# Output projection of the layers: one fp32 product against three products of high and low parts

## The reference, cut to what matters

```python
h = shift_token(x)
q, k, v = split(h @ wqkv)                  # 3 x 512 columns, 8 heads of 64
q, k = l2norm(q) * qs, l2norm(k) * ksc
q, k = rotary_xpos(q, k)
o = local_attention(q, k, v)               # windows of 128 tokens: own and previous
x = x + o @ wo                             # wo: 512 x 256, the product that is changed
h = layernorm(shift_token(x)) * lg + lb
h = h @ w1 + b1
x = x + (a * gelu(g)) @ w2 + b2
```

## Time and profile before

| | us |
|---|---|
| median of 3 runs (2383.41 to 2384.18) | 2384.12 |
| the profiled execution | 2385.16 |
| its span in the trace | 2383.4 |
| granted clock of PE, mean over the span | 0.982 |
| busy time PE / DVE / ACT / POOL | 2254.4 / 1928.0 / 1509.0 / 602.5 |

### The profile page before, as it was taken

One profiled execution on the slowest core, in us unless ns is written; L12 is line 12 of the kernel. 1 busy time (PEld: TensorE's weight loads), 2 busy tenths in 40 slices (PEclk: granted clock), 3 DMA queues, 4 the chain that ended last, 5 costly groups with the idle time before them and its releaser, 6 DMA issues. The chain is left out here.

```text
span 2383.4 us, 61531 instructions
## 1 busy us (share of the span) xinstructions
PE 2254.4 (95%) x21120; PEld 1735.2 (73%) x21120; DVE 1928.0 (81%) x4501; ACT 1509.0 (63%) x2970; POOL 602.5 (25%) x667
## 2 busy tenths in 40 slices
PE   6999999999999999789999998799999999987898
PEld 4776776777677766567777776688777777765787
DVE  6999799979998999678888886466688888873886
ACT  5777577757776777267767775344577776763343
POOL 1000000000000000145555552122355555441332
PEclk9999999999999999899999999899999999999999
DMA  4100100010011000300000000100100000001110
GB/s 127 34 13 20 60 15 14 19 60 15 19 50 42 15 20 19 122 1 1 9 0 9 1 8 1 56 0 0 50 1 8 1 9 0 9 1 36 54 35 27
DMA packets 67271, 58.43 MB, mean 25 GB/s; under 512 B 4069, under 2 KB 64605, under 8 KB 66913
## 3 DMA queue, kind: packets, MB, share of 16 engines
q1 hardware_dynamic: 67168, 57.07, 7.7%
HBM read 44.47 MB, written 8.40 MB: 22 GB/s over the span
## 5 line engine op out<-in xcount | busy, mean ns | idle before, releaser
L599 ACT ACTIVATE at_p<-at_ps_s,at_shift 128x1024 f32<-128x1024 f32 (+3 forms) x384 | 335.6, 899 | 90.6 <-PE at_ps_s L800 49.9
L340 DVE TENSOR_TENSOR at_p_lo<-at_p,at_p_hi 128x1024 f16<-128x1024 f32 (+3 forms) x384 | 356.9, 950 | 5.5
L1374 ACT ACTIVATE ly_probs<-ly_masked,ly_small,ly_rq 128x256 f32<-128x256 f32 x512 | 301.9, 595 | 8.4 <-DVE ly_small L1608 8.0
L1213 POOL TENSOR_TENSOR ly_rope_a<-ly_rope_a,ly_rope_t 128x512 f32<-128x512 f32 x128 | 163.6, 1278 | 318.7 <-DVE ly_rope_t L1576 318.7
L828 PE MATMUL at_ps_o<-at_v,at_p_hi 128*128 128x65 f16 x2304 | 238.4, 193 | 3.4 <-DVE at_p_lo L340 2.5
L828 PEld LDWEIGHTS at_ps_o<-at_v,at_p_hi 128*128 128x128 f16 x2304 | 210.8, 96 | 39.3 <-issue 26.8
L829 PE MATMUL at_ps_o<-at_v,at_p_hi 128*128 128x64 f16 x2304 | 237.5, 194 | 0.0
L830 PE MATMUL at_ps_o<-at_v,at_p_lo 128*128 128x65 f16 x2304 | 236.4, 192 | 0.0
L1605 DVE CUSTOM_DVE_ANT_0 ly_masked<-ly_ps,ly_mask 128x256 f32<-128x256 f32 x512 | 195.8, 419 | 48.8 <-PE ly_ps L1896 29.5
L335 DVE CAST at_p_hi<-at_p 128x1024 f16<-128x1024 f32 (+3 forms) x384 | 206.1, 554 | 25.9 <-ACT at_p L599 14.4
L1382 ACT ACTIVATE ly_operands_plain<-ly_ps 128x512 f32<-128x512 f32 x256 | 153.4, 599 | 112.8 <-PE ly_ps L1907 97.9
(11 more groups left out here) (241 smaller groups left out, 6230.5 us busy)
## 6 DMA issues: line engine op xcount, KB each, us to landing
at_w_raw<-in_Wv SPq DMA_DIRECT2D x32, 128.0 KB, 2.2
at_w_raw<-in_Wq SPq DMA_DIRECT2D x32, 128.0 KB, 2.3
at_w_raw<-in_Wk SPq DMA_DIRECT2D x32, 128.0 KB, 2.3
at_xio<-in_states SPq DMA_DIRECT2D x4, 1024.0 KB, 6.6
ly_a_raw<-x SPq DMA_DIRECT2D x8, 512.0 KB, 4.0
out<-stream SPq DMA_DIRECT2D x16, 256.0 KB, 2.2
ly_shifted<-stream SPq DMA_DIRECT2D x8, 508.0 KB
x<-at_xio SPq DMA_DIRECT2D x3, 1024.0 KB, 4.4
```

What stands on the lines that cost most here:

```text
L340: dve.tensor_tensor(p_lo[u % P_RING][:, :, off:], probs[u % P_RING][:, :, off:], p_hi[u % P_RING][:, :, off:], ALU.subtract).then_inc(p_lo ...
L599: act.activation(probs[u % P_RING][:, :, off:], ps_s[u % 2][:, :, off:], ACT.Exp, bias=shift[:], scale=SCORE_SCALE).then_inc(exp_done, 1)
L1213: pool.tensor_tensor(ra[:, i, :], ra[:, i, :], rt[:, i, :], ALU.add).then_inc(s["add_done"], 1)
L1374: step = act.activation(pr[:, j % 2, h, :], sm[:, j % 2, h, :], ACT.Exp, bias=small[:, j % 2, 1, h:h + 1], scale=rq[:, par, 2 * j + h:2 * ...
```

## The change

The output projection is done with three fp32r products per k-step instead of one fp32 product. For that

- wo is split into `wo_hi` and `wo_lo` once per layer, by POOL (`split_out_weights`, a cast and a subtraction of 128 x 1024) behind its tile 0; PE's wait ahead of tile 1 is for this split (`wo_done`) instead of for the transfer;
- DVE's `normalise_out` writes a plain `o_full`; ACT copies it to the high part (`high_out`, behind `exps(0)` of the next tile); POOL subtracts for the low part (`low_out`, first thing of the next tile, ahead of `add_rotated`); `oT_done` is now POOL's;
- PE does `project_out(t-1)` behind `project(t+2, 1)` instead of ahead of `probs_T(0)`;
- DVE does `add_attended(t-1)` behind `maxima(3)` instead of behind `maxima(2)`;
- a few semaphores that only ordered what was ordered anyway go, and buffers are laid out anew in the same memory.

```diff
+        wo_hi, o = cut(o + 8, LP, D)
...
-        oT, o = cut(o, LP, P, of=plain)
-        wo, o = cut(o, LP, D, of=plain)
+        oT, o = cut(o, 2, LP, P)
+        o_full, o = cut(o, LP, P, of=plain)
+        wo_raw, _ = cut(o, LP, D, of=plain)
+        wo_lo, o = cut(o, LP, D)
...
+                def low_out(g):
+                    hold(pool, s["tick"], (s["o_hi"], at(g + 1)))
+                    pool.tensor_tensor(oT[:, 1], o_full, f32(oT[:, 0]), ALU.subtract).then_inc(s["oT_done"], 1)
+
+                def split_out_weights(l):
+                    hold(pool, s["tick"], (s["ld_wo"], 16 * l + 16))
+                    pool.tensor_copy(wo_hi, wo_raw).then_inc(s["wo_hi"], 1)
+                    after(pool, "wo_hi", l + 1)
+                    pool.tensor_tensor(wo_lo, wo_raw, f32(wo_hi), ALU.subtract).then_inc(s["wo_done"], 1)
...
+                    if not first:
+                        low_out(nth(l, t) - 1)
                     if left >= 1:
                         add_rotated(l, t + 1, 0)
                         add_rotated(l, t + 1, 1)
...
-                        tile(l, t, t % 2, (t + 3) % TB)
+                        tile(l, t, t % 2, (t + 3) % TB, first=t == 0)
+                        if t == 0:
+                            split_out_weights(l)
...
+                def high_out(g):
+                    hold(act, s["tick"], (s["o_full"], at(g + 1)), (s["wo_mm"], at(g)))
+                    act.activation(oT[:, 0], o_full, ACT.Copy).then_inc(s["o_hi"], 1)
...
                     exps(l, t, 0, par)
+                    if not first:
+                        high_out(g - 1)
...
-                    after(dve, "wo_mm", g)
-                    dve.tensor_tensor(oT.rearrange("p j q -> p (j q)"), ps_pv[:], rT, ALU.mult).then_inc(s["oT_done"], 1)
+                    after(dve, "oT_done", g)
+                    dve.tensor_tensor(o_full.rearrange("p j q -> p (j q)"), ps_pv[:], rT, ALU.mult).then_inc(s["o_full"], 1)
...
                     maxima(l, t, 2, par)
-                    if not first:
-                        add_attended(l, t - 1)
                     if left >= 1:
                         rotate_k(l, t + 1, w)
                     maxima(l, t, 3, par)
+                    if not first:
+                        add_attended(l, t - 1)
...
-                        step = pe.matmul(ps_misc[:, 0:D], oT[:, k, :], wo[:, k, :], start=(k == 0), stop=(k == LP - 1),
-                                         skip_group_check=True)
+                        step = three_products(pe, ps_misc[:, 0:D], oT[:, 0, k, :], oT[:, 1, k, :], wo_hi[:, k, :], wo_lo[:, k, :],
+                                              k == 0, k == LP - 1)
...
-                    if not first:
-                        project_out(l, t - 1)
                     probs_T(g, 0)
                     if left >= 2:
                         project(l, t + 2, par, 1)
+                    if not first:
+                        project_out(l, t - 1)
                     probs_T(g, 1)
...
-                            hold(pe, s["tick"], (s["ld_wo"], 16 * l + 16))
+                            hold(pe, s["tick"], (s["wo_done"], at(l + 1)))
```

More of the change, by code:

```diff
@@ L1081, in phase_layers @@
                  "mx_done nb_done h_lo rc_done rB_done oT_done red_done fl_done ra_done kn_done kT_done xa_done msk "
-                 "kz_done ca_in ca_out pw_done add_done xs_done "
-                 "warmed bn ag vr nr xnd fT_mm ff_done f_hi f_lo gu_mm gl_done uf_done u_hi u_lo y_mm ya_done pw2 "
+                 "kz_done ca_in ca_out pw_done add_done xs_done o_full o_hi wo_hi wo_done "
+                 "bn ag vr nr xnd fT_mm f_hi f_lo gu_mm gl_done uf_done u_hi u_lo y_mm ya_done pw2 "
                  "b2_done z_gated z_done yg_done out_done tick")
@@ L1086, in phase_layers @@
         PE_SEMS = "xT_mm qkv_mm sc_mm pt_mm pv_mm qkT_mm rT_mm wo_mm fT_mm gu_mm y_mm"
[L1087 to L1090, removed]
+        ACT_SEMS = "o_hi h_hi ex_done sq_done pt_done rT_done qT_done v_done w_hi_done f_hi gl_done"
+        DVE_SEMS = ("mx_done nb_done h_lo rc_done rB_done o_full red_done fl_done ra_done kn_done kT_done xa_done msk "
+                    "w_lo_done bn ag vr nr xnd f_lo uf_done u_lo ya_done yg_done")
+        POOL_SEMS = "oT_done wo_hi wo_done aw_hi aw_done rope_next fw_hi fw_done xs_done kz_done ca_in ca_out pw_done add_done u_hi pw2 b2_done"
         def start(eng, which):
@@ L1186, in _ @@
                 pool.memset(f32(carry[:]), 0.0).then_inc(s["zeroed"], 1)
-                pool.memset(expo[:], -0.5).then_inc(s["const_done"], 1)
-                pool.wait_ge(s["zeroed"], 1)
+                pool.memset(expo[:], -0.5).then_inc(s["zeroed"], 1)
+                pool.wait_ge(s["zeroed"], 2)
                 def carry_in(l, t, par, w):
@@ L1237, in split_attention_weights, with tile @@
                     pool.tensor_tensor(a_lo[:, cols], a_raw[:, cols], f32(a_hi[:, cols]), ALU.subtract).then_inc(s["aw_done"], 1)
-                def tile(l, t, par, w, left=NT):
+                def low_out(g):
[6 more added lines that the diff above has]
+                    pool.tensor_tensor(wo_lo, wo_raw, f32(wo_hi), ALU.subtract).then_inc(s["wo_done"], 1)
+                def tile(l, t, par, w, left=NT, first=False):
+                    if not first:
+                        low_out(nth(l, t) - 1)
                     if left >= 1:
@@ L1256, in tile @@
                         inverse_deviation(l, 0)
+                    if left == 0:
+                        low_out(nth(l, t))
                 def chunk(l, c, left=NCH):
@@ L1384, in copy_reciprocals @@
                 def copy_reciprocals(g):
-                    hold(act, s["tick"], (s["rT_mm"], at(g + 1)), (s["oT_done"], at(g)))
+                    hold(act, s["tick"], (s["rT_mm"], at(g + 1)), (s["o_full"], at(g)))
                     act.activation(rT, ps_pt[:], ACT.Copy).then_inc(s["rT_done"], 1)
+                def high_out(g):
+                    hold(act, s["tick"], (s["o_full"], at(g + 1)), (s["wo_mm"], at(g)))
+                    act.activation(oT[:, 0], o_full, ACT.Copy).then_inc(s["o_hi"], 1)
                 def chunk_full(l, c, src):
@@ L1392, in chunk_full @@
                     for k in range(KT):
-                        step = act.activation(ffull[:, k, :], src[k][:], ACT.Identity,
+                        act.activation(ffull[:, k, :], src[k][:], ACT.Identity,
                                               scale=lncol[:, 0, k:k + 1], bias=lncol[:, 1, k:k + 1])
-                    step.then_inc(s["ff_done"], 1)
                 def chunk_hi(l, c, par, src):
@@ L1414, in u_high, with tile @@
                     act.activation(uT[rows_of, i, 0, :], uf[rows_of, i % 2, :], ACT.Copy).then_inc(s["u_hi"], 1)
-                def tile(l, t, par, slot, left=NT):
+                def tile(l, t, par, slot, left=NT, first=False):
                     g = nth(l, t)
                     exps(l, t, 0, par)
+                    if not first:
+                        high_out(g - 1)
                     if left >= 2:
@@ L1432, in tile @@
                     if left == 0:
-                        after(act, "warmed", 2 * l)
-                        act.activation(warm[:], expo[:, 0:1], ACT.Gelu).then_inc(s["warmed"], 1)
+                        act.activation(warm[:], expo[:, 0:1], ACT.Gelu)
                     copy_probs(g, 2)
@@ L1441, in tile @@
                     copy_reciprocals(g)
+                    if left == 0:
+                        high_out(g)
                     if left == 1:
@@ L1481, in last_chunk @@
                         return
-                    after(act, "warmed", 2 * l + 1)
-                    act.activation(warm[:], expo[:, 0:1], ACT.Exp).then_inc(s["warmed"], 1)
+                    act.activation(warm[:], expo[:, 0:1], ACT.Exp)
                     squares(l + 1, 0, 1)
@@ L1509, in _ @@
                     for t in range(2):
-                        tile(l, t, t % 2, (t + 2) % V_RING)
+                        tile(l, t, t % 2, (t + 2) % V_RING, first=t == 0)
                     with act.Fori(1, NT // 2 - 2) as i:
@@ L2120, in _ @@
                 scores(0, 0, 1, 0)
-                pe.wait_ge(s["zeroed"], B + 2)
+                pe.wait_ge(s["zeroed"], B + 3)
                 for l in range(L):
```

14 lines of the change are left out of this document (7 added, 7 removed).

## The result

| | before | after |
|---|---|---|
| median of 4 runs each, us | 2383.76 | 2516.75 (2515.93 to 2517.73) |
| span of the profiled execution, us | 2383.4 | 2514.9 |
| mean granted clock of PE | 0.982 | 0.98 |

The changed kernel is slower by a factor of 1.0558 (95% interval 1.054 to 1.0576), 133 us. The forecast was 2515 us.

A forecast was written before the change was run, and what follows sets the result against it. PE was taken to set the pace. Per tile -0.48 + 0.87 + 1.63 = +2.02 us, 117 us over 58 tiles, plus 13 for tile 1 and 1 for the last project_out: +131, 2515 us; range 2455 to 2555.

The forecast's parts named there:

- DVE's chain: DVE from scores 0 and 1 through L1588 to add_attended: makes K and qk_T(0) wait on PE; forecast's mechanism, chance 0.62.
- The sum's first two terms: PE per tile: -0.48 us from cheaper projection products, +0.87 us of new idle time ahead of K.
- the third term: PE ahead of qk_T(0): 1.63 us more idle per tile, waiting for DVE's late add_attended.
- PE's products: project_out on PE: twelve fp32r products take 1.36 us in place of 1.84, 0.48 us gained per tile.
- K's wait: PE ahead of K: with project_out moved, K waits for the normalised keys (L1588), 0.87 us idle per tile.
- The first small step behind POOL's add: DVE's first L1608, behind maxima(2): issued at 1114.11, blocked until POOL's add_rotated(0) ends at 1115.06.
- The first rival: DVE's first L1608 isn't blocked by POOL's add: +1.28 us per tile, 2472 us; chance 0.13.
- ACT: high_out on ACT: 0.63 us per tile, costed at nothing because ACT has 4 us of slack per tile.
- Tile 1: PE ahead of tile 1 waits for POOL's split of wo: 4.3 us idle per layer; 13 us together with its other costs.
- The clock rival: PE's gaps make its clock fall in every tile: up to 1.7 us per tile, 99 us more, 2613 us; chance 0.10.
- Only K's wait bites: Only PE's wait ahead of K costs: +0.39 us per tile, 2420 us; chance 0.05, shared with other slower sums under 2455.
- faster: Both PE waits are covered, so the products gain 30 us and tile 1's stall costs 12: 2366 us; chance 0.07.

The follow-up runs named there:

- e4: Changed kernel with DVE's add_attended between rotate_k and maxima(3), ahead of maxima(3) instead of behind it; 2459.7 us.
- e1: Changed kernel without POOL's low_out and without the product of the attended output's low part (8 products per tile in place of 12); 2475.9 us.
- e2: Kernel before, fp32 products and nothing split, with only the two moves: PE's project_out behind project(t+2, 1), DVE's add_attended behind maxima(3); 2462.2 us.
- e3: Changed kernel with the old PE and DVE order, without high_out and low_out, the high part standing in for the low part; 2378.2 us, ratio to before 0.9972.
- e5: Changed kernel with POOL's low_out between the two add_rotated instead of ahead of them; 2543.9 us.
- e9: Changed kernel with late wo wait, PE and ACT reordered against PE's waits at K and qk_T(0), and DVE's rotate_q ahead of normalise_out; 2419.1 us.
- e10: e9 with PE's stream_T behind values(2), and ACT's copy_probs(2) ahead of copy_queries and copy_probs(3) ahead of stream_hi; 2417.6 us.
- e6: Changed kernel with PE's wait for the split wo moved from ahead of tile 1 to just ahead of tile 1's project_out; 2510.0 us.

## Why the prediction was right, step by step

- **What set the time.** The forecast's step that mattered is DVE's chain: the small L1608 held by POOL's add, `add_attended` behind it, `qk_T(0)` behind that. It put `qk_T(0)` at 1118.36 - 1111.17 = 7.19 us behind the scores; measured were 7.03, released by `add_attended`. From there to the next scores it took 8.85 as before, measured 8.89. e4 moved `add_attended` and most of the wait went with it.
- **The sum's first two terms.** -0.48 and +0.87 are about right as intervals of PE (-0.41 and +0.81 in the tile shown), but neither counts in this kernel: `qk_T(0)` waits for DVE whatever PE saved or lost ahead of it, and the third term, 1.63, was simply what was left up to 1118.36. e1 and e2 show it: one has fp32r products, the other fp32, and `qk_T(0)` starts at 6.39 us in both. To say that the tile loses 0.87 at K and gets 0.48 back from the products is bookkeeping, not cause.
- **PE's products.** Forecast 1.36 us, measured 1.43 (1110.42 to 1111.85) in the changed kernel; 1.54 behind fp32 work (e3). The row of the feed-forward stage was one within a long run of equal products; the step in and out of such a run was not in it.
- **K's wait.** Forecast start 2.28 us behind the scores, measured 2.22, released by `normalise_keys`, and the same 2.22 in e2 without any of the new work. The move took away the cover, as said.
- **The first small step behind POOL's add.** Forecast blocked until the add ends, measured so: 0.94 us. Without `low_out` 0.17 (e1). The first rival, that it slips in, falls. It was also priced too low: by the same lock `rotate_k`, with both inputs in SBUF, would have waited in its place, as it does in e5. That its 2472 lies near e1's 2475.9 is because e1 takes the late add away.
- **The tile** was forecast at 16.04 us; 15.92 in the one shown, 15.96 as a mean.
- **ACT** was costed at nothing. In this order that holds: e1, with `high_out`, and e2, without it, have tiles of 15.34 and 15.32 us. In e9 and e10 it doesn't hold.
- **Tile 1.** Forecast a gap of 4.3 us from start to start; measured 3.74 of idle time, 3.99 counted as the forecast does (1037.42 to 1041.82, less the 0.41 that PE's last group takes). POOL's two splits of 128x1024 took 1.03 and 2.35 us, less than twice the rows of half the size. The clock did fall behind it, in both layers (0.55 over 1043 to 1045, 0.50 over 1786 to 1788). Among the middle tiles, with gaps of 0.8 and 1.5 us from start to start in every one, it stayed at 1.00 (1100 to 1480, 1870 to 2200). The clock rival falls.
- **The other rivals.** "Only K's wait bites" (2420) and "faster" (2366) needed `add_attended` 1.6 us or more sooner than the chain allowed; it wasn't. e3 shows how much there was to win had both waits been covered: 6 us.
- **The total** of 2515 against 2516.75 is closer than its terms, and that is luck. The middle tiles cost 58 x 1.95 = 113 us where 117 were forecast, so the edges cost some 20 where I had 14. e6 shows 7 of them at tile 1; the others I didn't take apart.

## What to carry to other kernels

Before moving a step behind another, ask what wait it was covering and who waits for it in turn: two moves, one on PE and one on DVE, cost more than half of the loss without any new work. When a queue has several waits, find the one that ends last: here PE's saving of 0.4 us and its wait of 0.8 both vanished in the wait for DVE. When an idle engine is given a new step, look at what it holds up: not only its own queue but every instruction of a neighbour that shares its access to memory, and put a number on it from a row where the two already met. And price a product at its place: twelve equal products in the middle of a long run of their kind are cheaper than the same twelve between others.

## What I had not expected of the hardware

Three fp32r products of 128x256 took 0.47 us right behind fp32 work and 0.35 otherwise (e3), and a group of twelve 1.43 us behind fp32r work (the changed kernel), 1.52 to 1.54 between fp32 groups (e10, e3). POOL's work grew less than in step with the size: the subtraction took 1.27 us for 128x512 and 2.35 for 128x1024, the cast 0.61 and 1.03.
